# Conv attention with routed experts on one core: five low parts made by GpSimd, four of them for steps that had a plain fp32 outward product

## The chip, the cores and the metric

The kernel runs on one NeuronCore of a Trainium2 chip. The metric is the device time of one execution in microseconds (us); before the change the median of three runs is 315.67 us (314.47 to 315.7). PE is TensorE's matmul, PEld its weight load, DVE is VectorE, ACT is ScalarE, POOL is GpSimd, SP is SyncE, whose queue issues most DMAs.

## What is computed

`x` is (4, 128, 32, 32): four batches of 128 channels by 1024 positions.

```python
x = x + nin(softmax(q k / sqrt(C)) v)           # group norm first; q, k, v, out are 128x128 products
t = to_tokens(x)                                # (4, 1024, 128)
t = t + linear_attention(layer_norm(t))         # 4 heads, softmax over positions on the keys
t = t + moe(layer_norm(t))                      # below
# _moe: 8 experts, top 2
logits = tokens @ router_w.T; probs = softmax(logits)
rw, re = top_k(probs, 2); rw = rw / rw.sum(-1)
for e in range(8):
    h = gelu(tokens @ w1[e] + b1[e])
    out = out + combine[:, e:e+1] * (h @ w2[e] + b2[e])
```

## The kernel before

The kernel is written by hand for five engine queues, each with its own instruction order and with semaphores between them. Four batches go through attention, linear attention and routing one behind the other; a batch's later stages are woven into the attention of the next. The last stretch, from about 195 us on, is the expert stage: 64 steps, numbered 0 to 63 here as in the code (`step`). Step `step` is batch `m = step // 16`, half `h` of 512 positions, and expert `e` (16 steps a batch: two halves by eight experts). The rest of the linear attention and routing of batches 2 and 3 is woven into these steps by the tables TAIL_AT and END_AT.

One expert step:

- PE `hidden`: `w1[e]` times the normed tokens `w` (wT_hi, wT_lo), three products of 128x512 (lines 1468 to 1470) into `scores`.
- ACT `gelu` (line 871) writes `gel`; DVE `weigh` (line 1354) multiplies it with the expert's share (broadcast rows that DMAs bring into `share_slot`, the tiles k_both, prob and pT_hi) into a slot of `hs_ring`, six slots in hs, h_f and hw.
- A split step: ACT `high` (line 882) rounds the slot to fp32r in `hs_hi[step % 8]` (halves of h_hi, q_hi and slices of pT_lo), and DVE `lower` (line 1363) subtracts it from the slot into `hs_lo[step % 8]`; then PE `outward` makes three products (1468 to 1470) into `ring`.
- A step in the set WHOLE: no `high`, no `lower`; PE multiplies the fp32 slot with the fp32 weight in one instruction (line 1831), which the trace shows as two records.

`outward` runs LAG = 5 steps behind `hidden`: on PE's queue stands hidden 36, outward 31, what the tables put at 36, hidden 37, outward 32, and so on. A lambda at number n in a table stands behind step n's own instructions, on every engine that has a part in it:

```python
END_AT = dict(ctx=24, m2=25, m3=27, o=29, st=29, w0=36, w1=37, lg=38, lT=39, rA=39, exp=39, rB=39, rC=39, z=42, c=42)
POOL_AT = dict(n2=2, n1=5, nr=12, ab=21, n2e=32, nre=38)
```

For the last batch that means: DVE takes the linear attention's output at 29 and gathers norm statistics (1102, 1106); POOL makes the reciprocal deviation (581, 583, 585) and the normed tile `w_n` in eight pieces (590), signalling `w_made` behind the fourth and the eighth (`second_norm`, n2e), and then adds `w_n` into t2 (601, `normed_residual`, nre, signal `z_made`). PE transposes the halves of `w_n` at 36 and 37 (1483), ACT and DVE split them (749, 1040), PE makes logits at 38 (1662, 1663) and transposes them at 39 (1671), DVE routes (1187 to 1224), PE transposes t2 and the shares at 42, ACT and DVE drain them (783, 1167), SP stores them (400, 407) and loads the broadcast shares back (441), and `weigh(48)`, the last batch's first, waits for those.

Of the kernel before, what the change touches and what calls it, by code (L numbers as in the profile page):

```python
# [23 lines left out]
FP32 = mybir.dt.float32  # L24
FP32R = mybir.dt.float32r
ALU = mybir.AluOpType
# [10 lines left out]
QUAD = BANK // P  # L37
# [40 lines left out]
LAG, HELD, RING, PARTED = 5, 8, 6, 2  # L78

POOL_AT = dict(n2=2, n1=5, nr=12, ab=21, n2e=32, nre=38)  # L80


WHOLE = frozenset((4, 6, 16, 18, 19, 20, 22, 28, 29, 30, 33, 34, 35, 37, 38, 40))


def splits_through(step):

    return sum(t not in WHOLE for t in range(step + 1))


LINEAR_CHAIN, ROUTING_CHAIN = 7, 18
# [42 lines left out]
def conv_attention_moe(nc, x, gn_scale, gn_bias, wq, bq, wk, bk, wv, bv, wp, bp,  # L134
# [8 lines left out]
    def loop_place(b):  # L143

        return Place(LOOP.banks, [n + (b - 2) * k for n, k in zip(before, loops)])
# [17 lines left out]
    with ctx:  # L163
# [3 lines left out]
        def sem(name):  # L167
            return ctx.enter_context(nc.semaphore(name))
# [73 lines left out]
        hs_hi = [m[:, n * BANK:(n + 1) * BANK] for m in (h_hi, q_hi) for n in range(2)]  # L242
        hs_lo = [m[:, n * BANK:(n + 1) * BANK] for m in (h_lo, q_lo) for n in range(2)]
# [9 lines left out]
        hs_ring = [m[:, n * BANK:(n + 1) * BANK] for m in (hs, h_f, hw) for n in range(2)]  # L253
# [46 lines left out]
        c_loaded = [sem(f"c_loaded{h}") for h in range(HALVES)]  # L300
        share_loaded = [sem(f"share_loaded{q}") for q in range(QUAD)]
        share_first = [sem(f"share_first{e}") for e in range(1, QUAD)]
        e_h, e_gelu, e_mul, e_hi, e_lo, e_y = (
            sem(n) for n in ("e_h", "e_gelu", "e_mul", "e_hi", "e_lo", "e_y"))
        stored = [sem(f"stored{h}") for h in range(HALVES)]
        last_out = sem("last_out")

# [3 lines left out]
        def gathered(*steps):  # L311

            found = {}
            for at, step in steps:
                found.setdefault(at, []).append(step)
            return found
# [4 lines left out]

        def wait_low(eng, step):

            eng.wait_ge(e_lo, splits_through(step))

        def first_batch(m):
            return isinstance(m, int) and m == 0
# [23 lines left out]
        def tile(m, j):  # L351

            return m[:, j * P:(j + 1) * P]
# [156 lines left out]
        def _(pool):  # L510
# [84 lines left out]
            def second_norm(lc):  # L595
                layer_norm(1, lc, t2, w_n, w_made)

            def normed_residual(lc):
                pool.wait_ge(w_made, lc * HALVES + HALVES)
                for n in range(PIECES):  # L600
                    last = pool.tensor_tensor(tiles_piece(t2, n), tiles_piece(t2, n), tiles_piece(w_n, n), ALU.add)
                last.then_inc(z_made, 1)
# [4 lines left out]
            def add_bout(lb, routed):  # L607
                if routed is not None:

                    wait_filled(pool, routed, "z1")  # L610
                for n in range(PIECES):
                    last = pool.tensor_tensor(tiles_piece(t2, n), tiles_piece(t1, n), tiles_piece(bout_b, n), ALU.add)  # L612
                last.then_inc(t1b_made, 1)
# [4 lines left out]
            for n in range(PIECES):  # L618
                last = pool.tensor_scalar(piece(h_f, n), piece(xb, n), gmul[:, 0:1], gadd[:, 0:1], ALU.mult, ALU.add)
# [18 lines left out]
            for n, (name, raw, hi, lo) in enumerate((("w1", w1_raw, w1_hi, w1_lo),  # L638
                                                    ("w2", w2_raw, w2_hi, w2_lo))):
                pool.wait_ge(ld_w[name], 16)  # L640
                for i in range(PIECES):
                    last = pool.tensor_scalar(piece(hi, i), piece(raw, i), 1.0, 0.0, ALU.mult, ALU.add)
                after(last)
                for i in range(PIECES):
                    last = pool.tensor_tensor(piece(lo, i), piece(raw, i), piece(hi, i).bitcast(FP32), ALU.subtract)
# [12 lines left out]
            def batch(place, b, la, lc):  # L658
                pool.wait_ge(x_again, b * 16)
                apart(pool)  # L660
                norm_x(b)
                add_bias(b)
                if place is SECOND:
                    group_rstd(SECOND, 2, B - 2, "gn_var2")
                if lc is not None:
                    second_norm(lc)
                    normed_residual(lc)
                first_norm(la)
                add_bout(la, place if lc is not None else None)
# [2 lines left out]
            pool.wait_ge(gn_made, 3)  # L672
            with pool.Fori(2, B) as b:
                batch(loop_place(b), b, b - 1, b - 2)
            norms = gathered(
                (POOL_AT["n2"], lambda: second_norm(B - 2)),
                (POOL_AT["n1"], lambda: first_norm(B - 1)),
                (POOL_AT["nr"], lambda: normed_residual(B - 2)),
                (POOL_AT["ab"], lambda: add_bout(B - 1, TAIL)),
                (POOL_AT["n2e"], lambda: second_norm(B - 1)),  # L680
                (POOL_AT["nre"], lambda: normed_residual(B - 1)),
            )
            for step in range(B * 2 * E):
# [4 lines left out]
        def _(act):  # L688
# [185 lines left out]
            def high(m, s):  # L874
                step = m * (2 * E) + s
                if step in WHOLE:
                    return
# [39 lines left out]
        def _(dve):  # L917
# [419 lines left out]
            def weigh(m, s):  # L1337
# [3 lines left out]
                before = step - RING  # L1341
                if before in WHOLE:

# [11 lines left out]

            def lower(m, s):
                step = m * (2 * E) + s
                if step in WHOLE:
                    return
                dve.wait_ge(e_hi, splits_through(step))  # L1360
                if m * (2 * E) + s >= HELD:
                    dve.wait_ge(e_y, m * (2 * E) + s + 1 - HELD)
                dve.tensor_tensor(hs_lo[s % HELD], hs_ring[step % RING], hs_hi[s % HELD].bitcast(FP32),
                                  ALU.subtract).then_inc(e_lo, 1)
# [548 lines left out]
```

## Time and profile before

| what | value |
|---|---|
| median of three runs | 315.67 us |
| the profiled execution | 317.83 us, span 316.0 us |
| PE busy | 301.5 us of the span |
| DVE, ACT, POOL busy | 256.2, 200.4, 156.9 us |
| mean granted TensorE clock | 0.988 of full |

The busy time of an engine is a sum over its instructions and says nothing of waits. The chain of work that ended last is followed back from the last instruction, at each step to what released it. POOL's busy time says little here either: what matters is when it works in the last 60 us.

### The profile page before, as it was taken

The numbers are of one execution on the slowest core, as the hardware profiler recorded it, in microseconds if no ns is written. First come the engines' busy times: TensorE is split into PE (matmuls) and PEld (weight loads), VectorE is DVE, ScalarE is ACT, GpSimd is POOL, SyncE is SP. The second block draws the span as 40 slices with busy tenths as digits, with TensorE's granted clock in tenths as the row PEclk, the third lists the DMA queues.
The fourth block names the chain that finished last, engine by engine and source line by source line (L and its number), as shares of the span: only waits on it lengthen the run. The fifth ranks groups of instructions, "written<-read, shape, count | busy, mean of one in ns | idle before, by whom it ended". The sixth has DMA issues, their size and how long they took to land.

```text
span 316.0 us, 5527 instructions
## 1 busy us (share of the span) xinstructions
PE 301.5 (95%) x1592; PEld 239.3 (76%) x1592; DVE 256.2 (81%) x641; ACT 200.4 (63%) x352; POOL 156.9 (50%) x357
## 2 busy tenths in 40 slices
PE   7998989989999999999999998999999999998996
PEld 5787768866878887878888796887776876666885
DVE  5598698587587798987698986999998897796996
ACT  3468473656771587664279576559777556785992
POOL 3898890149941985970684400399932069100000
PEclk9599999999999999999999999999999999999999
DMA  5902000020000021000000118295602881227911
GB/s 129 337 14 66 2 0 2 0 68 0 1 3 0 2 66 44 26 12 0 0 1 0 66 25 242 115 419 221 208 8 97 311 317 40 73 81 299 350 34 66
DMA packets 12904, 29.61 MB, mean 94 GB/s; under 512 B 2208, under 2 KB 6224, under 8 KB 10960
## 3 DMA queue, kind: packets, MB, share of 16 engines
q1 hardware_dynamic: 12448, 28.87, 26.4%
q10 hardware_dynamic: 432, 0.46, 0.4%
q8 instruction: 10, 0.16, 0.2%
q14 instruction: 14, 0.11, 0.1%
HBM read 24.73 MB, written 4.59 MB: 93 GB/s over the span
## 4 chain that ended last, share of the span: by engine, by line
PE 71%; DVE 14%; DMA 6%; issue 4%; ACT 3%; SPq 1%; DVEq 0%; ACTq 0%
PE ring L1483 10%; PE ring L1468 8%; PE ring L1470 8%; PE ring L1469 8%; PE scores L1468 7%; PE scores L1470 7%; PE scores L1469 7%; PE ring L1831 3%; DMA k_both<-scratch_s 3%; DVE pT_lo L1071 3%; DVE prob L1064 2%; PE ring L1648 2%; PE ring L1626 2%; PE ring L1613 2%; DMA scratch_c<-xT 1%
## 5 line engine op out<-in xcount | busy, mean ns | idle before, releaser
L871 ACT ACTIVATE gel<-scores,b_c 128x512 f32<-128x512 f32 x64 | 43.8, 685 | 18.7 <-PE scores L1470 15.0
L1071 DVE TENSOR_TENSOR pT_lo<-ring,pT_hi 128x512 fp32r<-128x512 f32 x64 | 40.5, 681 | 9.7 <-ACT pT_hi L730 9.5
L724 ACT ACTIVATE prob<-prob,row_max 128x1024 f32<-128x1024 f32 x32 | 36.8, 1150 | 11.5 <-DVE prob L1064 11.5
L581 POOL TENSOR_SCALAR rstd<-lmv 128x4 f32<-128x4 f32 x16 | 4.5, 283 | 76.1 <-DVE lmv L1106 74.8
L1064 DVE TENSOR_SCALAR_CACHE_REDUCE prob<-scores 128x1024 f32<-128x1024 f32 x32 | 38.7, 1216 | 3.4 <-PE scores L1470 2.9
L730 ACT ACTIVATE pT_hi<-ring 128x512 fp32r<-128x512 f32 x64 | 34.6, 599 | 9.2 <-PE ring L1483 8.9
L1483 PE MATMUL ring<-ident,prob 128*128 128x128 f32 x256 | 33.9, 275 | 3.4 <-DVE pT_lo L1071 2.1
L1483 PEld LDWEIGHTS ring<-ident,prob 128*128 128x128 f32 x256 | 28.7, 140 | 8.4 <-DVE pT_lo L1071 2.7
L1468 PE MATMUL scores<-wT_hi,w_hi 128*128 128x512 f32 x64 | 30.1, 470 | 1.7 <-ACT gel L871 1.7
L1468 PE MATMUL scores<-k_both,q_hi 128*128 128x512 f32 x64 | 27.0, 422 | 0.7 <-DVE prob L1064 0.7
L1468 PE MATMUL ring<-pT_hi,v_hi 128*128 128x512 f32 x64 | 26.6, 416 | 0.8 <-DVE pT_lo L1071 0.8
L1470 PE MATMUL scores<-k_both,q_lo 128*128 128x512 f32 x64 | 25.1, 393 | 0.0
L1470 PE MATMUL scores<-wT_hi,w_lo 128*128 128x512 f32 x64 | 25.1, 392 | 0.0
L1469 PE MATMUL scores<-wT_lo,w_hi 128*128 128x512 f32 x64 | 25.1, 392 | 0.0
L1469 PE MATMUL scores<-k_both,q_hi 128*128 128x512 f32 x64 | 25.1, 391 | 0.0
L1470 PE MATMUL ring<-pT_hi,v_lo 128*128 128x512 f32 x64 | 25.0, 391 | 0.0
L1469 PE MATMUL ring<-pT_lo,v_hi 128*128 128x512 f32 x64 | 25.0, 390 | 0.0
L734 ACT ACTIVATE o_s<-ring 128x512 f32<-128x512 f32 x8 | 4.8, 598 | 27.4 <-PE ring L1470 27.4
L590 POOL TENSOR_SCALAR u<-t,rstd 128x128 f32<-128x128 f32 x32 | 20.4, 654 | 0.9 <-POOL rstd L585 0.9
L612 POOL TENSOR_TENSOR t<-t,bout_row 128x128 f32<-128x128 f32 x32 | 14.0, 476 | 12.6 <-PE ring L1483 7.5
L590 POOL TENSOR_SCALAR w_n<-t,rstd 128x128 f32<-128x128 f32 x32 | 17.2, 551 | 0.9 <-POOL rstd L585 0.9
L1468 PEld LDWEIGHTS scores<-wT_hi,w_hi 128*128 128x128 f32 x64 | 12.1, 189 | 6.7 <-ACT gel L871 4.1
(304 smaller groups left out, 794.5 us busy)
## 6 DMA issues: line engine op xcount, KB each, us to landing
pT_hi<-scratch_s SPq DMA_DIRECT2D x8, 1024.0 KB, 7.4
prob<-scratch_s SPq DMA_DIRECT2D x4, 1024.0 KB, 7.6
k_both<-scratch_s SPq DMA_DIRECT2D x3, 1024.0 KB, 5.9
z_in<-scratch_z SPq DMA_DIRECT2D x8, 256.0 KB, 3.2
out_dram<-out_s SPq DMA_DIRECT2D x7, 256.0 KB, 2.4
xb<-in_x_dram SPq DMA_DIRECT2D x3, 512.0 KB, 3.2
scratch_z<-out_s SPq DMA_DIRECT2D x2, 512.0 KB, 2.8
k_both<-scratch_s SPq DMA_DIRECT2D x4, 256.0 KB, 5.5
```

Source lines behind the costliest of these rows:

```text
L590: last = pool.tensor_scalar(dst[:, j, :], src[:, j, :], neg[:, j:j + 1], std[:, j:j + 1], ALU.add, ALU.mult)
L612: last = pool.tensor_tensor(tiles_piece(t2, n), tiles_piece(t1, n), tiles_piece(bout_b, n), ALU.add)
L724: act.activation(prob[:, i % 2, :], prob[:, i % 2, :], ACT.Exp, bias=row_max[:, i:i + 1], scale=-1.0, accum_out=row_sum[:, 0, i:i + 1]).th ...
L730: act.activation(tile_group(pT_hi, n, i), as_tiles(ps(place, unit)), ACT.Copy).then_inc(p_hi_made, 1)
L871: act.activation(half(gel, s % 2), scores[:, s % 2, :], ACT.Gelu, bias=b1_c[:, s % E:s % E + 1]).then_inc(e_gelu, 1)
L1064: dve.tensor_scalar(prob[:, i % 2, :], scores[:, 2 * (i % 2):2 * (i % 2) + 2, :].rearrange("p a t -> p (a t)"), -SCALE, None, ALU.mult, AL ...
L1071: dve.tensor_tensor(tile_group(pT_lo, n, i), as_tiles(ps(place, unit)), tile_group(pT_hi, n, i).bitcast(FP32), ALU.subtract).then_inc(drai ...
L1468: pe.matmul(dst, lh, rh, start=start, stop=False)
L1469: pe.matmul(dst, lh, rl, start=False, stop=False)
L1470: return pe.matmul(dst, ll, rh, start=False, stop=stop)
L1483: last = pe.transpose(dst[0:t.shape[-1], j * step:j * step + rows], t, ident[0:rows, 0:rows])
L1831: last = pe.matmul(dst, tile(w2_s, e), hs_ring[step % RING], start=e == 0, stop=e == closing(m, h))
```

## The change

Steps 29, 33, 34 and 35 leave the set WHOLE, so they get a `high` on ACT, a low part, and three products on PE. Their low parts, and that of step 31, which DVE made before, are made by POOL in four pieces of 128x128, under a semaphore of their own, e_lo_pool. On POOL's queue those of 29 and 31 stand ahead of the last batch's `second_norm`, and those of 33, 34 and 35 between it and `normed_residual`. In the changed file the lines lie 9 lower in POOL's norm functions and 20 lower behind POOL's block (1468 is 1488, 590 is 599, 601 is 610), and 689 is the new subtraction.

```diff
-WHOLE = frozenset((4, 6, 16, 18, 19, 20, 22, 28, 29, 30, 33, 34, 35, 37, 38, 40))
+WHOLE = frozenset((4, 6, 16, 18, 19, 20, 22, 28, 30, 37, 38, 40))
+POOLED = (29, 31, 33, 34, 35)
...
+def lows_through(step):
+
+    return sum(t not in WHOLE and t not in POOLED for t in range(step + 1))
...
         def wait_low(eng, step):
 
-            eng.wait_ge(e_lo, splits_through(step))
+            if step in POOLED:
+                eng.wait_ge(e_lo_pool, POOLED.index(step) + 1)
+            else:
+                eng.wait_ge(e_lo, lows_through(step))
...
+            def lower(step):
+
+                pool.wait_ge(e_hi, splits_through(step))
+                pool.wait_ge(e_y, step + 1 - HELD)
+                for n in range(QUAD):
+                    last = pool.tensor_tensor(tile(hs_lo[step % HELD], n), tile(hs_ring[step % RING], n),
+                                              tile(hs_hi[step % HELD], n).bitcast(FP32), ALU.subtract)
+                last.then_inc(e_lo_pool, 1)
...
+                *((step, lambda step=step: lower(step)) for step in POOLED if step <= POOL_AT["n2e"]),
                 (POOL_AT["n2e"], lambda: second_norm(B - 1)),
+                *((step, lambda step=step: lower(step)) for step in POOLED if step > POOL_AT["n2e"]),
                 (POOL_AT["nre"], lambda: normed_residual(B - 1)),
...
-                if step in WHOLE:
+                if step in WHOLE or step in POOLED:
                     return
```

POOL's queue, from the end of batch 3's `add_bout` to the end of the program, before the change:

```order
L612 TENSOR_TENSOR t<-t,bout_row 128x128 x7
L581 TENSOR_SCALAR rstd<-lmv 128x4 [waits ln_stats1]
L583 TENSOR_SCALAR rstd<-lmv 128x4
L585 TENSOR_TENSOR rstd<-rstd,minus_half 128x4 [waits ln_small1]
...
L590 TENSOR_SCALAR w_n<-t,rstd 128x128 [waits ln_small1]
L590 TENSOR_SCALAR w_n<-t,rstd 128x128 x7
L601 TENSOR_TENSOR t<-t,w_n 128x128 [waits w_made]
L601 TENSOR_TENSOR t<-t,w_n 128x128 x7
```

The same place of the changed kernel:

```order
L621 TENSOR_TENSOR t<-t,bout_row 128x128 x7
L689 TENSOR_TENSOR pT_lo<-hw,pT_lo 128x128 [waits e_y,e_hi]
L689 TENSOR_TENSOR pT_lo<-hw,pT_lo 128x128 x3
L689 TENSOR_TENSOR pT_lo<-hs,pT_lo 128x128 [waits e_y,e_hi]
...
L590 TENSOR_SCALAR rstd<-lmv 128x4 [waits ln_stats1]
...
L599 TENSOR_SCALAR w_n<-t,rstd 128x128 x7
L689 TENSOR_TENSOR h_lo<-h_f,h_hi 128x128 [waits e_y,e_hi]
...
L689 TENSOR_TENSOR q_lo<-hw,q_hi 128x128 [waits e_y,e_hi]
...
L610 TENSOR_TENSOR t<-t,w_n 128x128 [waits w_made]
```

Eight subtractions (steps 29 and 31) came in ahead of the last norm, and twelve (33, 34, 35, the last two under the same names) between `w_n` and the sum with t2.

PE's queue from the transpose of the second half of `w_n` (at 37) to the transpose of the logits (at 39), before the change:

```order
L1483 MATMUL scores<-ident,w_n 128x128 [waits drained5,w_made]
...
L1831 MATMUL ring<-h_f,w_s 128x512 [waits e_mul]
L1662 MATMUL ring<-wT_hi,router_two 128x512 [waits drained0,drained4]
...
L1662 MATMUL ring<-wT_hi,router_two 128x512 [waits drained1,drained5]
...
L1831 MATMUL ring<-hw,w_s 128x512 [waits e_mul]
L1671 MATMUL scores<-ident,p 128x16 [waits drained4,drained0,drained1]
```

The same place of the changed kernel:

```order
L1503 MATMUL scores<-ident,w_n 128x128 [waits drained5,w_made]
...
L1488 MATMUL ring<-h_hi,w_hi 128x512 [waits e_lo_pool]
L1489 MATMUL ring<-h_lo,w_hi 128x512
L1490 MATMUL ring<-h_hi,w_lo 128x512
L1682 MATMUL ring<-wT_hi,router_two 128x512 [waits drained0,drained4]
...
L1682 MATMUL ring<-wT_hi,router_two 128x512 [waits drained1,drained5]
...
L1488 MATMUL ring<-q_hi,w_hi 128x512 [waits e_lo_pool]
...
L1691 MATMUL scores<-ident,p 128x16 [waits drained4,drained0,drained1]
```

The outward products of steps 33 (ahead of the logits) and 34 (ahead of the transpose of the logits) waited for DVE's `weigh` before and wait for POOL's subtraction now.

## Rows read from the trace of the kernel before

**Rows 1.** The page: busy us and share by engine; the chain by engine.

```profile
PE 301.5 (95%) x1592; PEld 239.3 (76%) x1592; DVE 256.2 (81%) x641; ACT 200.4 (63%) x352; POOL 156.9 (50%) x357
...
PE 71%; DVE 14%; DMA 6%; issue 4%; ACT 3%; SPq 1%; DVEq 0%; ACTq 0%
```

**Rows 2.** The chain that ended last, 257 to 260 us: start us, us, what.

```profile
257.68 0.86 PE ring L1831 x2
258.54 0.23 PE scores L1468
...
259.24 0.86 PE ring L1831 x2
```

**Rows 3.** The same chain, 263 to 293 us.

```profile
263.30 0.44 PE scores L1483 x4
...
267.54 0.69 DVE wT_lo L1040
...
269.70 0.86 PE ring L1831 x2
270.56 0.61 PE scores L1671 x8
271.19 0.30 DVE logit L1187
...
276.47 0.06 DVE comb L1224
...
280.79 0.45 SPq L407
...
281.29 3.83 DMA scratch_c<-xT
...
285.26 4.75 DMA k_both<-scratch_s
...
292.12 0.50 PE scores L1468
```

**Rows 4.** ACT's timeline: start us, us, instruction, count, [idle us before it <- releaser].

```profile
253.64 0.69 ACT L871 ACTIVATE gel<-scores,b_c 128x512 f32<-128x512 f32 x1 [2.49 <-PE scores L1470]
...
257.47 0.63 ACT L882 ACTIVATE pT_lo<-hs 128x512 fp32r<-128x512 f32 x1 [0.42 <-DVE hs L1354]
...
260.84 0.69 ACT L871 ACTIVATE gel<-scores,b_c 128x512 f32<-128x512 f32 x1 [0.87 <-DVE hw L1354]
262.39 0.69 ACT L871 ACTIVATE gel<-scores,b_c 128x512 f32<-128x512 f32 x1 [0.87 <-PE scores L1470]
```

**Rows 5.** DVE's timeline at the steps around 31.

```profile
258.13 0.69 DVE L1363 TENSOR_TENSOR pT_lo<-hs,pT_lo 128x512 fp32r<-128x512 f32 x1
258.74 0.69 DVE L1354 TENSOR_TENSOR h_f<-gel,k_both 128x512 f32<-128x512 f32 x1
...
263.12 0.77 DVE L1354 TENSOR_TENSOR hs<-gel,prob 128x512 f32<-128x512 f32 x1 [0.86 <-ACT gel L871]
```

**Rows 6.** POOL's timeline, its last work of the program.

```profile
255.18 0.43 POOL L581 TENSOR_SCALAR rstd<-lmv 128x4 f32<-128x4 f32 x1 [16.05 <-DVE lmv L1106]
...
259.27 5.36 POOL L590 TENSOR_SCALAR w_n<-t,rstd 128x128 f32<-128x128 f32 x8 [0.22 <-POOL rstd L585]
264.72 4.71 POOL L601 TENSOR_TENSOR t<-t,w_n 128x128 f32<-128x128 f32 x8
```

**Rows 7.** POOL's pieces: duration ns min/median/max, by line and tile.

```profile
L564 POOL TENSOR_TENSOR h_lo<-h_f,h_hi x24: 450/460/465, 40.7 to 137.4; 128x128 fp32r<-128x128 f32 x24
L590 POOL TENSOR_SCALAR w_n<-t,rstd x8: 442/656/995, 259.3 to 264.2; 128x128 f32<-128x128 f32 x8
```

**Rows 8.** POOL's timeline of the norms before, and busy us by stretch there.

```profile
211.55 0.19 POOL L581 TENSOR_SCALAR rstd<-lmv 128x4 f32<-128x4 f32 x1
...
215.93 10.02 POOL L590 TENSOR_SCALAR u<-t,rstd 128x128 f32<-128x128 f32 x8 [0.22 <-POOL rstd L585]
...
216.00:218.00 2.00, 2.00 (x10) 1.60 (x10) 2.00 (x4) 1.74 (x4) 2.00 (x2) 1.00 0.00 0
```

**Rows 9.** Stretches: us, PE PEld DVE ACT POOL busy (x), PEclk, DMA, GB/s.

```profile
9.00:10.00 1.00, 1.00 (x3) 0.81 (x4) 0.76 (x3) 0.00 (x0) 0.94 (x2) 0.50 1.11 352
...
14.00:15.00 1.00, 1.00 (x4) 0.71 (x3) 0.47 (x2) 0.69 (x1) 1.00 (x3) 0.50 1.15 348
...
290.00:292.00 2.00, 0.79 (x4) 0.32 (x2) 1.86 (x4) 1.14 (x2) 0.00 (x0) 1.00 1.07 438
```

More of the change, by code:

```diff
@@ L302, in conv_attention_moe @@
         share_first = [sem(f"share_first{e}") for e in range(1, QUAD)]
-        e_h, e_gelu, e_mul, e_hi, e_lo, e_y = (
-            sem(n) for n in ("e_h", "e_gelu", "e_mul", "e_hi", "e_lo", "e_y"))
+        e_h, e_gelu, e_mul, e_hi, e_lo, e_lo_pool, e_y = (
+            sem(n) for n in ("e_h", "e_gelu", "e_mul", "e_hi", "e_lo", "e_lo_pool", "e_y"))
         stored = [sem(f"stored{h}") for h in range(HALVES)]
```

## The prediction

> **What bounds the kernel now.** I read the page first. It shows PE busy for 95% of the span and leading the chain of waits with 71% of it [rows 1]; the reader is to see that microseconds of PE count, unless something else is last at that place. So I read the chain in order of time around steps 28 to 52. Up to the transpose of the first half of `w_n` (263.30 to 263.74) it is PE back to back. From there the chain is another one: logits, their transpose at 270.56, routing on DVE from 271.19 to 276.5, the drains, the store issued at 280.79 with 3.83 us, the share load with 4.75 us, and only then weigh 48, its gelu, and hidden 52 at 292.12 [rows 3]. Between 290 and 292 us PE is busy for 0.79 of 2.00 [rows 9]: it has run out of work. Hence a delay at the transpose of the logits goes one for one into the end, because nothing between it and 292.12 has slack, and time saved on PE behind it only lengthens PE's wait.
>
> Then I read POOL. It waits 16.05 us for the last batch's statistics, begins at 255.18, needs 4.09 us for both halves' small instructions, makes `w_n` from 259.27 for 5.36 us and sums from 264.72 to 269.43 [rows 6]. Four pieces are half of 5.36, so the first `w_made` comes near 262.0 and the second at 264.6. PE wants the first at 263.3 [rows 3]: 1.3 us of slack. The second is wanted at about 264.96, 0.3 us of slack. `z_made` is wanted only at 276. POOL is half idle on the whole and tight just here.
>
> **The change part by part.**
>
> PE: a plain product takes 0.86 us in the chain, three products 3 x 0.23 = 0.69 [rows 2]. Four steps save 4 x 0.17 = 0.7 us, of which 0.17 (step 29) lies ahead of the transpose at 36.
>
> ACT: four more `high` at 0.63 [rows 4], 2.5 us. That of 29 stands behind gelu 30 (253.64 to 254.33) and ends at 254.9, in the hole ahead of gelu 31. Those of 33 to 35 stand behind gelu 34, 35 and 36, and ACT idles 0.87 us ahead of each of two of these gelus [rows 4]. I cost them at nothing. Without that hole each would push a gelu by up to 0.6 us, and PE's hidden two steps on.
>
> DVE: loses the low part of 31, 258.13 to 258.74 (0.6 us) [rows 5]. The next weigh starts at 258.74 when its gelu is ready anyway, and DVE waits for ACT again at 263.12 [rows 5]. Gain: nothing.
>
> POOL gets 20 pieces of the very kind that `norm_x` runs, fp32r out of two fp32 tiles: 0.450 to 0.465 us each over 24 of them [rows 7]. That is 1.84 us for a step undisturbed. But `w_n`'s pieces spread from 0.442 to 0.995 with a median of 0.656 while DVE multiplies two SBUF tiles [rows 7], and eight pieces of `u` took 10.02 us, 1.25 each, where DVE was busy for all of the time [rows 8]. So a step of four costs between 1.84 us and 4 x 1.25 = 5.0 us. I take 0.55 a piece, 2.2 us, where DVE is partly idle, and 0.7, 2.9 us, for step 31, beside which DVE runs without a break.
>
> Here a rule can be weighed. The Trainium skill (GPSIMD Engine Reference, Performance versus the Vector engine) gives 4497 ns for an fp32 addition of 2048 columns; a quarter of it, 1.12 us a step, is an estimate from that page. By it POOL's chain would shrink so far that PE's own order would set the transpose of the logits, at 271.4, and the loss would be 0.8 us. The row on pieces of 128 columns is of this kernel and goes into the sum: 1.84 us at least.
>
> Now POOL's queue in its new order.
> - Low 29: starts at 254.9, ends at 257.1 (2.2). PE wants it at 259.24 [rows 2]: hidden. The norm, though, could have started at 255.18.
> - Low 31: its `high` is over at 258.10 [rows 4], since ACT makes it only behind gelu 32. POOL's queue stands idle from 257.1 to 258.2, with the norm behind it, whose statistics are ready. This head-of-line wait is the heart of the forecast. It ends at 258.2 + 2.9 = 261.1.
> - Small instructions of both halves, 4.1 [rows 6] (4.38, from 211.55 to 215.93, is the other bound [rows 8]): 265.2, where before `w_n` began at 259.27.
> - `w_n`: DVE soon has nothing to do, so 0.5 a piece: the first half at 267.2, the second, with DVE back, at 269.4. Before: 262.0 and 264.6.
> - Low 33: 271.6. Low 34: 273.8. Low 35: 276.0. The sum with t2, 4.71 [rows 6]: 280.7.
>
> PE in its order: out 31 is over at 263.3 - 0.2 (the saving of step 29) = 263.1, and PE waits for `w_made` until 267.2, 4.1 us. Transpose, hidden 37, outward 32: 0.44 + 0.69 + 0.69 gives 269.0; the second transpose goes at 269.4 and, with hidden 38, ends at 270.5. Outward 33 waits for its low part until 271.6, ends at 272.3. Logits 0.5 and hidden 39: 273.5; outward 34 waits until 273.8, ends at 274.5. The transpose of the logits starts at 274.55 where it started at 270.56 [rows 3]: 4.0 us late. ACT and DVE split the second half of `w` meanwhile; by their durations that is done near 271.6, ahead of the logits' turn.
>
> Behind it: DVE's route takes as long as before, its shares come at 276.5 + 4.0 = 280.5. PE wants `z_made` at about 280.0 and gets it at 280.7, transposes until 281.7; ACT drained z 2.5 us behind the end of the route before, so it wants it at 283. Hidden by 1 us. POOL's last pieces lie beside weigh 40 and 41 and may stretch them, 0.3 us. Store and share load are unchanged, the tail from 292.12 too. The sum: 4.0 + 0.3 = 4.3 us. The profiled execution would take 317.83 + 4.3 = 322.1; it stood 2.2 us above the median, and 315.67 + 4.3 is **320.0 us**.
>
> Bounds. Best case: pieces at 0.46 and `w_n` at 0.442. Then POOL has low 34 at 258.2 + 1.84 + 4.1 + 3.54 + 3.68 = 271.4, and the transpose starts near 272.4: +1.9, 317.5 us. Worst case of the plain mechanism: low parts at 3.7 us (0.93 a piece, near the maximum of `w_n`), 4.4 of small instructions, 5.4 of `w_n`: 258.2 + 3 x 3.7 + 9.8 + 0.7 = 279.8, +9.2.
>
> **The rivals.**
>
> A, the forecast: the norm waits behind low 31, and low 33 and 34 hold PE. +2 to +6, 317.7 to 321.7. Chance 0.52.
>
> B, the same, and TensorE's clock falls. Nowhere in this stretch does PE idle for more than 1.34 us, and the clock there is granted at 1.00 [rows 9]; a wait of 4 us is new. At the start of the program, behind short waits and small products, it stood at 0.50 (1.2 GHz) from 9 to 15 us [rows 9]. If it does so from 267 on for as long, PE's work between the waits doubles: 0.88, 1.38, 1.38, 0.88, 1.38, 1.38 brings outward 33 to 274.5, then 0.5, 0.69 and 0.69 the transpose to 276.4. That is 1.8 us more than A, 321.8 us; a shorter fall is covered by the waits for POOL. Chance 0.24. The Trainium skill (TensorE: Matmul & The Clock Gate, HAM oscillation) says that gaps in TensorE's work put it back to the lower clock; the stretch at 290 us, with its clock at 1.00, shows that a short one does not.
>
> C, the shared port: every low piece costs like `u`, 1.25 us, since DVE's multiplications run beside it [rows 8]. Low 31, 33 and 34 at 5.0, the rest as in the sum: 258.2 + 15 + 8.3 + 0.7 = 282.2, 11.6 late; against it speaks that DVE is starved while PE waits. Half-way between, some +8, 323.7 us. Chance 0.10. The Trainium skill (SBUF — State Buffer, SBUF: two separate sides) calls the port pair that VectorE and GpSimd share an exclusive lock for instructions with two SBUF inputs; the spread of the `w_n` pieces agrees.
>
> D, no change. The delay of the norm would have to stay within the 1.3 and 0.3 us that PE leaves it, or the share load would have to take it up. The chain of waits has no gap there [rows 3]. It would give 315.5 us. Chance 0.07.
>
> E, faster: PE bounds throughout and keeps the 0.7 us of the cheaper products, 315.0 us or, with what DVE and the drains give, 314 us. It decides only if low 31 ends before the norm's first statistics at 255.18, or if POOL's pieces ran at under a third of the shortest row. Its `high` ends at 258.10, so I see no way but an error in my reading of which step stands where. Chance 0.05. The last 0.02 is for losses above C.
>
> **How the numbers follow.** The likeliest is A at 320.0. The range drops D and E below and half of C above: 317.7 to 323.2. About 0.5% (1.6 us) is what a measurement of this kernel tells from no change, so slower begins at 317.3: A, B, C and the rest, 0.88. Same 0.08, faster 0.04.
>
> **What would show it.** In the changed profile: POOL idle for about 1 us between low 29 and low 31 and `w_n` starting near 265; PE waiting about 4 us for `w_n` at 263 and then for line 689 ahead of outward 33 and 34; the transpose of the logits near 274.5; route, store and load of unchanged length behind it; hidden 52 near 296.4; granted clock 1.00 from 266 to 276 for A, 0.50 in part of it for B. Pieces of line 689 at 0.46 undisturbed and up to 0.9 beside DVE; near 1.25 for C. The prediction is wrong if `w_n` starts before 262, if the delay at the transpose of the logits does not arrive at 292.12, or if ACT's four rounds push gelus.

## The result and the profile after

The changed kernel takes 328.9 us (median of five runs, 327.34 to 330.05) against 315.67 us (five runs of before, 314.47 to 318.25): 1.0403 times as long, interval 1.0358 to 1.0448. The forecast was 320.0. The profiled execution took 330.05 us, with a span of 328.3 us and a mean granted clock of 0.964. A few executions of the runs further down took some per cent longer than the others of the same kernel, and all medians and ratios given here leave them out.

POOL first, since the forecast was built on its queue. Its timeline in the changed kernel:

```profile
254.96 2.21 POOL L689 TENSOR_TENSOR pT_lo<-hw,pT_lo 128x128 fp32r<-128x128 f32 x4 [15.75 <-ACT pT_lo L902]
258.46 2.61 POOL L689 TENSOR_TENSOR pT_lo<-hs,pT_lo 128x128 fp32r<-128x128 f32 x4 [1.29 <-ACT pT_lo L902]
...
265.19 3.45 POOL L599 TENSOR_SCALAR w_n<-t,rstd 128x128 f32<-128x128 f32 x8 [0.22 <-POOL rstd L594]
268.61 1.71 POOL L689 TENSOR_TENSOR h_lo<-h_f,h_hi 128x128 fp32r<-128x128 f32 x4
270.27 3.37 POOL L689 TENSOR_TENSOR q_lo<-hw,q_hi 128x128 fp32r<-128x128 f32 x8
273.60 3.32 POOL L610 TENSOR_TENSOR t<-t,w_n 128x128 f32<-128x128 f32 x8
```

This is the predicted queue within 0.3 us: 1.29 us idle ahead of low 31 (1.1 forecast), and `w_n` at 265.19 where 265.2 was forecast (259.27 before [rows 6]). From there POOL is even faster than forecast, and from 265.19 to 276.92 it runs 28 pieces without one wait.

The changed kernel's PE timeline:

```profile
266.98 0.66 PE L1503 MATMUL scores<-ident,w_n 128*128 128x128 f32 x4 [3.83 <-POOL w_n L599]
...
272.51 0.40 PE L1683 MATMUL ring<-wT_lo,router_top 128*128 128x512 f32 x1
279.33 0.79 PE L1682 MATMUL ring<-wT_hi,router_two 128*128 128x512 f32 x1 [6.42 <-DVE wT_lo L1060]
...
283.04 1.03 PE L1691 MATMUL scores<-ident,p 16*128 16x16 f32 x8
```

The wait of 3.83 us for `w_n` was forecast. The second one, 6.42 us ahead of the second half's logits, was not, and its releaser is DVE and not POOL. Before, the same places looked like this:

```profile
268.26 0.50 PE L1662 MATMUL ring<-wT_hi,router_two 128*128 128x512 f32 x1 [0.68 <-DVE wT_lo L1040]
...
270.49 0.66 PE L1671 MATMUL scores<-ident,p 16*128 16x16 f32 x8
```

The wait was 0.68 us, and the transpose of the logits began at 270.49. Now it begins at 283.04, 12.6 us later, and the span is 12.3 us longer (328.3 against 316.0): the whole loss lies ahead of it.

So the changed kernel's DVE timeline has to be read around 269 us:

```profile
268.31 0.69 DVE L1060 TENSOR_TENSOR wT_lo<-scores,wT_hi 128x512 fp32r<-128x512 f32 x1 [4.63 <-ACT wT_hi L769]
269.16 8.32 DVE L1374 TENSOR_TENSOR hs<-gel,prob 128x512 f32<-128x512 f32 x1 [0.16 <-ACT gel L891]
277.40 0.68 DVE L1383 TENSOR_TENSOR pT_lo<-hs,pT_lo 128x512 fp32r<-128x512 f32 x1
278.00 0.68 DVE L1395 TENSOR_TENSOR out_s<-ring,z_in 128x512 f32<-128x512 f32 x1
278.60 0.67 DVE L1060 TENSOR_TENSOR wT_lo<-scores,wT_hi 128x512 fp32r<-128x512 f32 x1
```

One multiplication, `weigh(37)`, is recorded with 8.32 us. Others of its shape take 0.69 to 0.77 [rows 5]. It ends at 277.48, 0.56 us behind POOL's last piece (276.92). DVE is "busy" in every busy-time row of that stretch, though the work is that of 0.69 us. Behind it come a low part, an output sum and then the split `wT_lo` that PE's second logits wait for.

The clock, in the changed kernel's windows (columns as in [rows 9]):

```profile
266.00:268.00 2.00, 1.02 (x7) 0.93 (x8) 0.00 (x0) 0.32 (x1) 2.00 (x6) 1.00 0.00 0
268.00:270.00 2.00, 2.00 (x8) 1.54 (x7) 1.53 (x2) 1.48 (x3) 2.00 (x6) 0.53 0.00 0
...
272.00:274.00 2.00, 0.91 (x4) 0.39 (x3) 2.00 (x1) 1.06 (x2) 2.00 (x5) 1.00 0.00 0
274.00:276.00 2.00, 0.00 (x0) 0.00 (x0) 2.00 (x1) 0.00 (x0) 2.00 (x6) 0.74 0.00 0
276.00:278.00 2.00, 0.00 (x0) 0.00 (x0) 2.00 (x2) 0.00 (x0) 0.92 (x3) 0.50 0.00 0
...
288.00:290.00 2.00, 2.00 (x8) 1.54 (x7) 1.79 (x8) 0.69 (x1) 0.00 (x0) 0.85 0.00 0
```

The clock falls twice to the lower level (0.50, 1.2 GHz): the first time about 1 us behind the end of the wait of 3.83 us, the second time while PE stands in the wait of 6.42 us. At the lower level PE's products start 0.43 us apart (279.92 and 280.35) where they started 0.23 apart before [rows 2].

The pieces of the new subtraction by themselves, in the changed kernel (the line's summary, ns min/median/max):

```profile
L689 POOL TENSOR_TENSOR q_lo<-hw,q_hi x8: 454/458/465, 270.3 to 273.2; 128x128 fp32r<-128x128 f32 x8
...
L689 POOL TENSOR_TENSOR pT_lo<-hs,pT_lo x4: 459/680/912, 258.5 to 260.2; 128x128 fp32r<-128x128 f32 x4
```

While `weigh(37)` stands still, POOL is not slowed at all: 454 to 465 ns, as its undisturbed pieces had [rows 7]. Low 29 and low 31, beside which DVE gets its turns, each have pieces that take about twice as long, up to 954 and 912 ns.

### The profile page after: what moved, and what is told of

It is laid out like the page before. It is cut to its first block, busy times and chain, and to the rows that moved or that the text cites. A ratio compares the mean times of both kernels' runs of the same rounds, so it can differ in the third digit from the quotient of the medians.

```text
span 328.3 us, 5567 instructions
## 1 busy us (share of the span) xinstructions
PE 306.0 (93%) x1596; PEld 244.7 (75%) x1596; DVE 263.8 (80%) x640; ACT 202.5 (62%) x356; POOL 163.6 (50%) x377
## 4 chain that ended last, share of the span: by engine, by line
PE 60%; DVE 13%; issue 11%; POOL 10%; ACT 2%; DMA 2%; SPq 1%; DVEq 0%; POOLq 0%
PE ring L1503 10%; PE ring L1488 7%; PE ring L1490 7%; PE ring L1489 7%; PE scores L1488 6%; PE scores L1490 6%; PE scores L1489 6%; POOL u L599 3%; DVE pT_lo L1091 3%; DVE prob L1084 2%; PE ring L1851 2%; POOL w_n L599 2%; PE ring L1646 2%; PE ring L1633 2%; POOL rstd L594 2%
## 5 line engine op out<-in xcount | busy, mean ns | idle before, releaser
L1490 PE MATMUL scores<-wT_hi,w_lo 128*128 128x512 f32 x64 | 26.0, 407 | 0.0
L1489 PE MATMUL scores<-wT_lo,w_hi 128*128 128x512 f32 x64 | 26.0, 406 | 0.0
L621 POOL TENSOR_TENSOR t<-t,bout_row 128x128 f32<-128x128 f32 x32 | 14.0, 474 | 12.6 <-PE ring L1503 7.5
L594 POOL TENSOR_TENSOR rstd<-rstd,minus_half 128x4 f32<-128x4 f32 x16 | 16.6, 1038 | 0.0
L599 POOL TENSOR_SCALAR w_n<-t,rstd 128x128 f32<-128x128 f32 x32 | 15.2, 490 | 0.9 <-POOL rstd L594 0.9
```

What stands on the lines that cost most here:

```text
L594: pool.tensor_tensor(std[:, tiles], std[:, tiles], minus_half[:, tiles], ALU.pow).then_inc(ln_small[n], 1)
L599: last = pool.tensor_scalar(dst[:, j, :], src[:, j, :], neg[:, j:j + 1], std[:, j:j + 1], ALU.add, ALU.mult)
L1489: pe.matmul(dst, lh, rl, start=False, stop=False)
L1490: return pe.matmul(dst, ll, rh, start=False, stop=stop)
```

## The experiments

**How they are compared.** The place of the loss is known, so each run is also measured there: the time on PE from the end of outward 31 to the start of the transpose of the logits, by the timeline. It is 7.20 us in before (263.29 to 270.49) and 19.89 us in after (263.15 to 283.04). The other columns give the duration of `weigh(37)`, PE's waits in the stretch (for `w_n`, for low 33 or ahead of the second logits), and the median less that of before on the same chip. The stretch is read from one execution of each kernel.

| run | stretch, us | less before's | weigh 37, us | PE's waits, us | median less before's |
|---|---|---|---|---|---|
| after | 19.89 | +12.7 | 8.32 | `w_n` 3.83, logits 6.42 | +13.2 |
| e1_29_31_only | 12.16 | +5.0 | 0.84 | `w_n` 3.82 | +6.1 |
| e2_33_34_35_only | 7.20 | 0.0 | 0.85 | low 33 1.02 | +0.9 |
| e3_all_on_dve | 9.70 | +2.5 | 0.69 | `w_n` 2.04 | +1.3 |
| e4_sum_waits | 14.96 | +7.8 | 4.06 | `w_n` 3.83, logits 2.42 | +5.6 |
| e5_wait_before_33 | 12.01 | +4.8 | 0.84 | `w_n` 3.84, logits 0.45 | +5.6 |
| e6_wait_each_low | 12.34 | +5.1 | 0.73 | `w_n` 3.91 | +3.3 |
| e9_29_31_on_dve | 8.03 | +0.8 | 0.96 | `w_n` 0.15, low 33 1.21 | +1.8 |
| e10_wait_and_busy | 11.51 | +4.3 | 0.69 | `w_n` 0.17 (filled), low 33 1.28 | +4.1 |
| e11_pe_kept_busy | 19.12 | +11.9 | 8.45 | `w_n` 0.18 (filled), low 33 0.22, logits 1.99 | +11.2 |

The third column gives the last within 1.2 us, but for e4 and e6, where it lies 2.2 and 1.8 us above it. The time from the transpose of the logits to the end of the span hardly moves (45.5 us in before, 45.3 in after).

### e1_29_31_only and e2_33_34_35_only: the change in two parts

```diff
-WHOLE = frozenset((4, 6, 16, 18, 19, 20, 22, 28, 30, 37, 38, 40))
-POOLED = (29, 31, 33, 34, 35)
+WHOLE = frozenset((4, 6, 16, 18, 19, 20, 22, 28, 30, 33, 34, 35, 37, 38, 40))
+POOLED = (29, 31)
```

> Steps 33, 34 and 35 keep their plain product and have no low part; POOL makes those of 29 and 31 alone. Theory P (the long multiplication on DVE, weigh 37 with 8.3 us, is starved of the SBUF port by POOL's twenty two-input pieces in a row, and ends when that row ends): the row behind w_n is eight pieces again, weigh 37 takes at most 4 us, and what remains is the late norm, w_n some 6 us later: 4 to 6 us over the kernel before, 320 to 322 us. Rival W (weigh 37 is long because of something that it waits for and that has to do with the late norm): weigh 37 stays near 8 us and the time near 328 us.

Measured: 322.38 us against 316.29, 1.0183 (1.0105 to 1.026). PE waits 3.82 us for `w_n`, and `weigh(37)` takes 0.84 us. This is the forecast's late norm, with no starved DVE. POOL's timeline of this run:

```profile
264.57 3.45 POOL L599 TENSOR_SCALAR w_n<-t,rstd 128x128 f32<-128x128 f32 x8 [0.22 <-POOL rstd L594]
268.10 4.28 POOL L610 TENSOR_TENSOR t<-t,w_n 128x128 f32<-128x128 f32 x8
```

Here the sum with t2 stands directly behind `w_n`, and its first instruction waits for `w_made`, which `w_n`'s last piece gives: it starts 3.53 us behind `w_n`'s start, where low 33 in after starts 3.42 behind it (268.61 less 265.19). So POOL stands still for a moment between the two. e5 below shows what that moment is worth.

```diff
-WHOLE = frozenset((4, 6, 16, 18, 19, 20, 22, 28, 30, 37, 38, 40))
-POOLED = (29, 31, 33, 34, 35)
+WHOLE = frozenset((4, 6, 16, 18, 19, 20, 22, 28, 29, 30, 37, 38, 40))
+POOLED = (33, 34, 35)
```

> Step 29 keeps its plain product and DVE makes the low part of 31, so the norm on POOL is as early as before. Theory P: low 33 starts near 264.7 and twenty two-input pieces follow without a gap until about 273; the weigh that comes into them (near 265.2) takes until 273, some 8 us, and the time is 6 to 9 us over before, 322 to 325 us. Rival W (it has to do with the late norm): no weigh over 1.5 us, only outward 33 waits a little: within 2 us of before, 316 to 318 us.

Measured: 317.17 us against 316.29, 1.0024 (0.9977 to 1.0071), no difference. POOL's and DVE's timelines of this run:

```profile
258.21 5.38 POOL L599 TENSOR_SCALAR w_n<-t,rstd 128x128 f32<-128x128 f32 x8 [0.22 <-POOL rstd L594]
263.57 2.60 POOL L689 TENSOR_TENSOR h_lo<-h_f,h_hi 128x128 fp32r<-128x128 f32 x4
266.13 3.84 POOL L689 TENSOR_TENSOR q_lo<-hw,q_hi 128x128 fp32r<-128x128 f32 x8
```

```profile
264.14 0.85 DVE L1374 TENSOR_TENSOR hs<-gel,prob 128x512 f32<-128x512 f32 x1
264.91 0.94 DVE L1383 TENSOR_TENSOR pT_lo<-hs,pT_lo 128x512 fp32r<-128x512 f32 x1
```

Twenty two-input pieces follow each other here too (twelve lows, then the sum), and DVE gets in each time. So it isn't the length of the row from DVE's request on, as I had thought, and that theory fell. What differs is what stands ahead: `w_n` took 5.38 us, since DVE took turns in it, where it took 3.45 undisturbed in after. Neither half alone has the starved DVE. In e2 turns of DVE break POOL's row. In e1 the row is unbroken through `w_n`, but the sum's wait for `w_made` breaks it there. In after the lows stand between the two, and when the sum comes its wait has long been met and breaks nothing.

### e3_all_on_dve: the splits without POOL

```diff
-POOLED = (29, 31, 33, 34, 35)
+POOLED = ()
```

> All five low parts on DVE, as split steps are elsewhere; POOL has none. By all theories no stall at the port and an early norm: PE saves 4 x 0.17 us, DVE has 4 x 0.6 us more in a stretch in which it waits for ACT. Expected within 1.5 us of before, 314.5 to 317 us. If ACT's four extra roundings were the cost, it would be 2 us or more above.

Measured: 317.56 us against 316.29, 1.0025 (0.9981 to 1.007), no difference. POOL's and PE's timelines show why the four times 0.17 us of PE don't come out as a gain:

```profile
259.01 6.93 POOL L599 TENSOR_SCALAR w_n<-t,rstd 128x128 f32<-128x128 f32 x8 [0.22 <-POOL rstd L594]
264.29 0.66 PE L1503 MATMUL scores<-ident,w_n 128*128 128x128 f32 x4 [2.04 <-POOL w_n L599]
```

DVE's low parts of 33, 34 and 35 (at 260.29, 261.59 and 262.89) run beside `w_n`, which takes 6.93 us instead of 5.36 [rows 6], and PE waits 2.04 us for it. The clock then falls to 0.50 (266 to 268 us). So the stretch is 2.5 us longer than before's in that execution, whatever the cheaper products save.

### e4_sum_waits: POOL's row cut ahead of the sum

```diff
+                (POOL_AT["nre"], lambda: wait_drained(pool, END, "w1")),
                 (POOL_AT["nre"], lambda: normed_residual(B - 1)),
```

> The changed kernel, with POOL's sum of t2 and w_n held back until the second half of w is split, so that POOL's row of two-input pieces stops behind low 35 (273.6). Theory P: weigh 37 ends about 0.6 us behind that, near 274.2, with 5.0 us instead of 8.3; the time falls by about 3.3 us to 325.5 us. Rival W: weigh 37 stays at 8.3 us, and since the sum then waits for what weigh 37 holds back, the time rises to 329 us or more.

Measured: 321.91 us against 316.29, 1.0216 (1.0126 to 1.0305). DVE's and POOL's timelines:

```profile
267.06 4.06 DVE L1375 TENSOR_TENSOR hs<-gel,prob 128x512 f32<-128x512 f32 x1 [0.68 <-ACT gel L892]
```

```profile
267.19 3.38 POOL L689 TENSOR_TENSOR q_lo<-hw,q_hi 128x128 fp32r<-128x128 f32 x8
273.00 4.21 POOL L610 TENSOR_TENSOR t<-t,w_n 128x128 f32<-128x128 f32 x8 [2.43 <-DVE wT_lo L1061]
```

`weigh(37)` ends at 271.12, 0.55 us behind POOL's last low piece (270.57). Counted from the start of `w_n` (265.19 in after, 262.11 here), the row's end moved from 11.73 to 8.46 us and the stall's end from 12.29 to 9.01, both by 3.3 us. The stall lasts until POOL stops, not for a time of its own. The size expected for it was 5.0 us, it was 4.06.

### e5_wait_before_33 and e6_wait_each_low: POOL waits for itself

```diff
+                (33, lambda: pool.wait_ge(w_made, B * HALVES)),
```

```diff
                 last.then_inc(e_lo_pool, 1)
+                pool.wait_ge(e_lo_pool, POOLED.index(step) + 1)
```

The first edit is e5's, the second e6's. e5 has one wait more than after, between the last piece of `w_n` and low 33, on the signal that this piece itself gives. No other order, size or place changes.

> The changed kernel; POOL waits for its own last w_n piece to be complete before it issues low 33, and for nothing else. Theory S (POOL's pieces, issued one behind the other with no wait on a completed one, run into each other so that the port is never free; a wait on the own completion sets them level again): weigh 37 comes in soon after such a wait, takes its turn as in the runs in which it took 0.85 us, and the time falls to 320 to 323 us, what the late norm and the waits for low 33 and 34 cost. Rival L (only the length of POOL's row counts: any row of two-input pieces holds DVE off until it ends): weigh 37 stays at 8 us, 328 us.

Measured: 321.88 us against 316.31, 1.0172 (1.0079 to 1.0265). DVE's and POOL's timelines:

```profile
270.33 0.84 DVE L1375 TENSOR_TENSOR hs<-gel,prob 128x512 f32<-128x512 f32 x1 [0.68 <-ACT gel L892]
```

```profile
265.39 3.45 POOL L599 TENSOR_SCALAR w_n<-t,rstd 128x128 f32<-128x128 f32 x8 [0.22 <-POOL rstd L594]
268.92 1.71 POOL L689 TENSOR_TENSOR h_lo<-h_f,h_hi 128x128 fp32r<-128x128 f32 x4
270.59 4.74 POOL L689 TENSOR_TENSOR q_lo<-hw,q_hi 128x128 fp32r<-128x128 f32 x8
```

The wait costs POOL some 0.1 us (low 33 begins 3.53 us behind `w_n`'s start, 3.42 in after) and takes 7.5 us off `weigh(37)`. From here to the second logits DVE has its turns, and POOL pays for them (4.74 us for the eight pieces instead of 3.37).

> The changed kernel; POOL waits for its own completion behind each low part, not ahead of low 33. Theory S: weigh 37 comes into low 33 as before, is held until the wait behind it (270.3), 1 to 2 us in all, and the time is 320 to 324 us. Rival L: a wait of some 0.1 us on a completed piece does not free the port for DVE, weigh 37 stays at 8 us and the time at 328 us.

Measured: 319.6 us against 316.31, 1.0146 (1.0033 to 1.0259). `weigh(37)` arrives at 267.46, in the fourth piece of low 33, and takes 0.73 us, since that low ends 0.19 us later (267.65) and POOL's wait comes behind it. The 1 to 2 us expected for it were too much.

### e9_29_31_on_dve: POOL keeps only 33 to 35

```diff
-POOLED = (29, 31, 33, 34, 35)
+POOLED = (33, 34, 35)
```

> The changed kernel, but DVE makes the low parts of 29 and 31, so that POOL's norm is early; 33, 34 and 35 stay on POOL, 29 is split. By both theories of the stall it depends on whether DVE's multiplications meet POOL's pieces at work when they come; with w_n broken up by DVE's own instructions, as in the run with 33, 34 and 35 alone, no long weigh is expected: within 1.5 us of before, 315 to 318 us.

Measured: 318.14 us against 316.31, 1.0058 (1.0007 to 1.0108). With nothing ahead of the norm PE waits 0.15 us for `w_n`, and the late norm and the starved DVE are gone together. What is left of the loss, 0.8 us in the stretch, goes with a wait of 1.21 us for low 33.

### e10_wait_and_busy and e11_pe_kept_busy: the share of the clock

Both give PE products that nobody reads, so that it doesn't stand still: 16 of them ahead of the wait for `w_n`, and in e11 24 more ahead of the second logits. e10 is e5 with the 16, e11 is after with both.

```diff
             def turn_w(place, lb, n):
+                if place is END and n == 0:
+                    dst = open_unit(place, "w0")
+                    for _ in range(16):
+                        pe.matmul(dst, router_top[:, :], half(v_lo, 0), start=True, stop=True)
                 pe.wait_ge(w_made, lb * HALVES + n + 1)
```

> POOL's wait ahead of low 33, and 16 products that nobody reads ahead of PE's wait for the first half of w_n. The clock stays at 1.00 from 266 to 270 us, where it stood at 0.50; the second transpose of w_n comes at about 269.1 in place of 270.4, and some 1 us is saved: 320 to 321.5 us, still 3 us or more above before, since the late norm stays.

Measured: 320.45 us against 316.39, 1.0107 (1.0029 to 1.0185). The clock stays at 1.00 in every window from 262 to 290 us. This is after with neither starved DVE nor fallen clock, and it takes what A forecast (320.0). The 16 products save 0.5 us of the stretch (12.01 less 11.51) where some 1 us was expected: `weigh(37)` now comes earlier, DVE's turns stretch low 33 (2.66 us, 1.71 in e5), and PE waits 1.28 us for it.

> The changed kernel with products that nobody reads put in ahead of PE's two long waits: 16 of 128x512 ahead of the wait for the first half of w_n, 24 ahead of the second logits. Theory S and a clock that falls when TensorE has nothing to do: the clock stays at 1.00, weigh 37 stays at 8 us (its stall ends with POOL's row), and what is saved is that logits, hidden 39 and outward 34 run at 0.23 us a product in place of 0.43: 2 us, 326.5 to 327.5 us. If the clock were the main part of the loss, the time would fall by 5 us or more.

Measured: 327.55 us against 316.39, 1.03 (1.0201 to 1.04), at the upper end of the expected. e11's windows:

```profile
266.00:268.00 2.00, 1.81 (x11) 1.25 (x10) 0.00 (x0) 0.60 (x1) 2.00 (x6) 1.00 0.00 0
...
280.00:282.00 2.00, 2.00 (x7) 1.12 (x5) 0.50 (x1) 1.67 (x3) 0.00 (x0) 0.54 0.68 188
```

The first fall is gone; the second still came, from 280 to 287 us, behind a wait of 1.99 us that the products left. So e11 prices only part of the clock. The rest can be read from the same eight products and their transpose, second logits to transpose of the logits: 1.94 us in e10 at the full clock (274.53 to 276.47), 2.85 in e11, 3.71 in after (279.33 to 283.04). The second fall costs after 1.8 us there. The first costs 0.5 us, net of the new wait for low 33 (the stretch of e5 less that of e10).

### m1_port_trials and m2_port_trials: POOL's row and one DVE instruction, by themselves

Both are before with trials behind the end of the computation. In a trial POOL issues a row of pieces: first some with one tensor input (like `w_n`), then some with two (like the lows). One piece's completion releases DVE's multiplication of 128x512 out of two SBUF tiles, which arrives about 0.08 us into the next piece. Such a multiplication takes 0.68 us alone.

```diff
+                for n in range(ones):
+                    last = pool.tensor_scalar((w_n, p1T)[n // TILES][:, n % TILES, :], t1[:, n % TILES, :], ..., ALU.add, ALU.mult)
+                for n in range(twos):
+                    last = pool.tensor_tensor(..., t1[:, n % TILES, :], t2[:, n % TILES, :], ALU.subtract)
+                    if n == go:
+                        last.then_inc(tr_go, 1)
...
+                dve.wait_ge(tr_go, k + 1)
+                    dve.tensor_tensor(half(hw, 0), half(gel, 0), other, ALU.mult).then_inc(tr_dve, 1)
```

> The kernel before with fourteen trials behind its end, in each of which VectorE and GpSimd alone work: POOL issues some one-input pieces (w_n's kind) and then two-input pieces (the low parts' kind), and one multiplication of 128x512 on DVE is released by the completion of a given piece. Theory S: released early in a row (piece 2) it takes 0.8 to 1 us; behind 8 one-input pieces, or late in a row of 20, it takes until the row ends (3 to 6 us); a wait on the own completion ahead of it makes it short again; with one operand in PSUM it takes 0.7 us anywhere. Rival L: it is held until the row ends from any release. Rival D (DVE always gets its turn behind at most one piece when nothing else runs, and the long one in the changed kernel had another cause): 0.8 to 1.1 us in all trials.

> The kernel before with fourteen other trials behind its end. Theory S: the multiplication on DVE waits for the end of POOL's row if about 11 or more pieces of 128 columns have gone by since POOL's last wait on a completed one, and takes 0.93 us below that; the edge is between 10 and 14 pieces. One-input pieces ahead count like two-input ones, so that 4 of them with release by the first two-input piece give 0.93 us, 8 give 5.06 us as before, 6 either. POOL instructions of 512 columns: some 1.4 us each; few instructions, so DVE gets its turn behind one (up to 2.3 us). Two multiplications behind each other in a held trial: the first is held until the row ends, the second takes 0.7 us. A one-input VectorE instruction has not been tried; if it needs the shared port it is held too.

Measured, one execution each (these kernels' whole times, 428.19 and 431.02 us, mean nothing). "Arrives in" counts the row's pieces.

| POOL's row | DVE arrives in | DVE's instruction, ns |
|---|---|---|
| 16 or 20 two-input | 3rd, 7th, 11th, 12th, 13th, 14th | 924 to 926 |
| 20 two-input | 15th | 2993 |
| 20 two-input | 17th | 2157 |
| 20 two-input, POOL waits for its own 8th piece | 11th | 926 |
| 20 two-input; DVE reads PSUM for one operand | 11th | 689 |
| 2 or 4 one-input, then 12 two-input | 4th, 6th | 925 |
| 6 one-input, then 12 two-input | 8th | 5036 |
| 8 one-input, then 12 two-input | 10th (three trials) | 5035 to 5056 |
| the same | 14th | 3406 |
| the same, POOL waits for its own 8th piece | 10th | 926 |
| 8 one-input, then 12 two-input; DVE reads PSUM for one operand | 10th | 689 |
| one-input alone | 5th, 13th | 692 (POOL's piece 992, 997) |
| 5 and 6 two-input of 128x512 | 2nd, 5th | 1733, 1734 |
| 8 one-input, then 5 two-input of 128x512 | 10th | 5394 |
| 8 one-input, then 12 two-input; DVE's is a one-input multiplication | 10th | 4771 |
| 8 one-input, then 12 two-input; two multiplications one behind the other | 10th | 5036, then 679 |

Two trials of m1 next to each other, DVE's and POOL's timelines; the second differs by the wait alone:

```profile
347.22 5.06 DVE L1482 TENSOR_TENSOR hw<-gel,prob 128x512 f32<-128x512 f32 x1 [4.10 <-POOL u L706]
356.50 0.93 DVE L1482 TENSOR_TENSOR hw<-gel,prob 128x512 f32<-128x512 f32 x1 [4.22 <-POOL u L706]
```

```profile
343.30 3.47 POOL L698 TENSOR_SCALAR w_n<-t,rstd 128x128 f32<-128x128 f32 x8 [0.72 <-DVE hw L1482]
346.73 3.35 POOL L706 TENSOR_TENSOR u<-t 128x128 f32<-128x128 f32 x8
350.03 1.70 POOL L706 TENSOR_TENSOR uT<-t 128x128 f32<-128x128 f32 x4
352.46 3.47 POOL L698 TENSOR_SCALAR w_n<-t,rstd 128x128 f32<-128x128 f32 x8 [0.72 <-DVE hw L1482]
356.01 3.79 POOL L706 TENSOR_TENSOR u<-t 128x128 f32<-128x128 f32 x8
```

The starved one ends at 352.28, 0.55 us behind POOL's last piece (351.73), as in after. When DVE is served, POOL's row stretches by 0.44 us; when it isn't, POOL loses nothing.

What follows. It is all or nothing: DVE is served behind the current piece, or behind the row. Which of the two is settled by what POOL has run without a wait or a turn for DVE until then: arriving in the 14th two-input piece it was served, in the 15th and the 17th it was not, and with one-input pieces ahead the change lies between four and six of them. The order of arrival inside a piece is no cause, since all trials arrive at the same point. A wait counts only if POOL has to stand in it, as behind its own last piece. The operand in PSUM takes the multiplication out of it altogether, so what DVE waits for lies in its reading from SBUF. The expectations for m1 and m2 held but for two sizes: the edge in a row of two-input pieces lies at 15 and not between 10 and 14, and POOL's instructions of 512 columns hold DVE until their row ends too when 8 one-input pieces stand ahead (5394 ns).

## Why the prediction was wrong

**The late norm: right, and sized right.** Low 31 began at 258.46 (258.2 forecast), `w_n` at 265.19 (265.2), PE waited 3.83 us (4.1). With the rest switched off, e10's stretch is 4.3 us longer than before's, where A said 4.0, and its median lies 4.1 us above. One term of A's sum is too small: it takes 0.5 us for the logits, which are four products of 0.23 us, 0.9 us. In A's own sum all but 0.1 us of that disappears in the wait for low 34.

**The price of a piece: right, a bit high.** Low 29 took 2.21 us (2.2), low 31 2.61 (2.9), low 33 1.71 (2.2), `w_n` 3.45 (some 4.2). Low 33 was over at 270.3 instead of 271.6, and outward 33 waited for nothing of POOL's in after.

**B, the clock: it fell, twice.** The first fall, behind the wait for `w_n`, cost 0.5 us instead of 1.8. A second fall, behind a wait that the forecast did not have, cost 1.8.

**The step that failed** is this one: "ACT and DVE split the second half of `w` meanwhile; by their durations that is done near 271.6, ahead of the logits' turn." It was done at 279.3. The forecast took DVE's durations from before, where POOL's rows were broken up, and put them beside a POOL that runs 28 pieces in a row. DVE's `weigh(37)` stands ahead of that split on its queue and took 8.32 us. C had the port in it, but with the loser the wrong way round: it priced what DVE does to POOL (1.25 us a piece) and gave nothing to what POOL does to DVE. "Against it speaks that DVE is starved while PE waits" was said of a lack of work, and it is just this lack that made POOL's row unbroken: DVE idled 4.63 us ahead of 268.31, so no turn of its own fell into `w_n`. So the late norm, which the forecast had, set up the starved DVE, which it had not.

**The sum, as measured.** Late norm 4.3, first fall of the clock 0.5, second fall 1.8, and the starved DVE itself the rest of 12.7 us, 6.1. The terms are differences between kernels, and the last is what remains. By e5 the two last terms go with one wait: 19.89 less 12.01, 7.9 us.

**Port or not.** The Trainium skill (SBUF — State Buffer, SBUF: two separate sides) says that whichever of the two engines' instructions starts first holds the shared pair for the whole of it and the other blocks. The short cases agree (in m2 the piece of POOL's at DVE's turn reads 902 ns, the others 446 to 454). The page speaks of single instructions and says nothing of a row of them: by it `weigh(37)` would have waited for the piece under way, of 0.46 us, and it waited for that one and eighteen more.

**What stays open** is how POOL keeps the pair from one piece to the next. Pieces start every 0.41 us and are recorded with 0.45 to 0.47, so they overlap; in m1's starved row of two-input pieces the record grows from 455 ns at its head to 476 at its end, and behind a wait or a turn for DVE it is back at 447 to 455. GpSimd's cores drifting apart until one of them always holds the pair would fit. The Trainium skill (GPSIMD Engine Reference, Instruction dispatch) says that consecutive instructions are no barrier between its cores. But m2's starved rows show no growth (452 to 454 ns), so this is not shown. Nor do the runs say why six one-input pieces count for as much as thirteen with two inputs: behind six and one with two inputs DVE was starved, behind thirteen with two inputs it was not.

**Tail.** "Store and share load are unchanged" was wrong for the store: from its issue to its landing `scratch_c<-xT` took 3.83 us before [rows 3] and 2.1 us in after and in e10; the load of k_both took 4.75 us before and 4.5 in after. So the shares come earlier behind the routing, and PE's wait of 1.34 us behind them is gone in both. What that gives back is spent elsewhere: on products at the lower clock in after (until 288.4 us), and in e10 partly on waits of 0.62, 0.51 and 0.43 us at three earlier places. The time from the transpose of the logits to the end came out nearly the same (45.3 us, 45.5 before); that it agrees so closely is no merit of the forecast. Why the store was quicker was not looked into.

## What to carry to other kernels

Before a step goes to POOL's queue, look at what stands behind it: low 31 waits for a rounding on ACT, and the norm behind it was ready 3 us earlier; that alone cost 4 us to spare PE 0.7. When POOL gets many short instructions without a wait between them, put in a wait on the completion of its own last one (0.1 us here); a wait for something long done breaks nothing. Or keep in the order that one which is there already, as the sum's wait did in e1, or let the DVE instruction beside it read one operand from PSUM. Break the row where an important DVE step falls. And a busy row of 8 us for an instruction that elsewhere takes 0.7 is a wait; look through the durations of single instructions, not only for idle times. No version beat the kernel before: e2 and e3 can't be told from it, and the others' intervals lie above it (e9's by a hair, from 1.0007).

## What the runs showed of the hardware beyond that

- A DVE multiplication of one SBUF tensor by a constant was starved as well (4.77 us), while one with two tensors, one of them in PSUM, was not (0.689 us). The Trainium skill (SBUF — State Buffer, SBUF: two separate sides) counts DVE's two-port mode among the users of the shared pair; whether that instruction ran in it no run here shows.
- POOL's one-input pieces alone did not hold DVE up in the two trials (0.692 us beside them), but six of them ahead were enough for the two-input ones to do it.
- The granted clock fell with waits of 3.83 and 6.42 us in after, with one of 2.04 us in e3, and in e11 behind one of 1.99 us that followed 24 products. It held through one of 1.34 us in before [rows 9] and one of 2.42 us in e4, whose windows from 270 to 280 us all show 1.00. So the length of one wait alone does not settle it in these runs.
